# Output blocks inside key blocks, layer norm work in odd steps, and another order at the end of the attention part

## The reference

```
x = L0_attn_x
x = x + _L0_attn_ref(_layernorm(x, axis=-1), L0_attn_gamma, L0_attn_w_qkv, L0_attn_w_out)
x = x + _L0_ffn_ref(_layernorm(x, axis=-1), L0_ffn_router_w, L0_ffn_w1, L0_ffn_b1, L0_ffn_w2, L0_ffn_b2)
...
# _L0_attn_ref
xn = rms_norm(x, gamma)
qkv = xn @ w_qkv
...
sim = jnp.einsum('bhid,bhjd->bhij', q * scale, k)
attn = jax.nn.softmax(sim, axis=-1)
out = jnp.einsum('bhij,bhjd->bhid', attn, v)
...
# _L0_ffn_ref
expert_out = jnp.matmul(jax.nn.gelu(jnp.matmul(xt, w1) + b1), w2) + b2
out = expert_out * jnp.sum(combine, axis=-1, keepdims=True)
```

## Time and profile before

| | before |
|---|---|
| time, median of 3 runs (lowest to highest) | 1206.61 us (1205.59 to 1207.03) |
| the profiled execution: its own time, its span | 1207.99 us, 1206.2 us |
| busy in the span: TensorE, its weight loads | 1166.3 us (97%), 990.5 us (82%) |
| VectorE, ScalarE, GpSimd | 1008.0 us (84%), 872.4 us (72%), 660.9 us (55%) |
| mean granted TensorE clock | 0.997 |
| chain that ended last, share of TensorE | 83% |

### The profile page before, as it was taken

One profiled execution on the slowest core, in us unless ns is written; L12 is line 12 of the kernel. 1 busy time (PEld: TensorE's weight loads), 2 busy tenths in 40 slices (PEclk: granted clock), 3 DMA queues, 4 the chain that ended last, 5 costly groups with the idle time before them and its releaser, 6 DMA issues.

```text
span 1206.2 us, 26861 instructions
## 1 busy us (share of the span) xinstructions
PE 1166.3 (97%) x10171; PEld 990.5 (82%) x10171; DVE 1008.0 (84%) x1738; ACT 872.4 (72%) x1897; POOL 660.9 (55%) x826
## 2 busy tenths in 40 slices
PE   9999999999999999999999999999999988999999
PEld 6778888888788888887888788878887876898898
DVE  7888888888988888888888988898889877777764
ACT  6888877888788778877888788878887866334432
POOL 5776565655565555655565556565655576222321
PEclk9999999999999999999999999999999989999999
DMA  4232112311231123112311222121212234424421
GB/s 133 78 90 74 36 36 71 86 30 36 62 88 36 37 71 89 36 37 71 89 37 36 71 70 56 36 65 51 71 35 63 54 88 139 131 90 135 129 73 36
DMA packets 58271, 82.95 MB, mean 69 GB/s; under 512 B 12576, under 2 KB 34592, under 8 KB 58144
## 3 DMA queue, kind: packets, MB, share of 16 engines
q1 hardware_dynamic: 58144, 81.24, 24.5%
HBM read 31.14 MB, written 16.25 MB: 39 GB/s over the span
## 4 chain that ended last, share of the span: by engine, by line
PE 83%; DVE 7%; issue 2%; POOL 1%; ACT 1%; DMA 1%; SPq 0%; ACTq 0%; POOLq 0%
PE ps L609 43%; PE ps L688 18%; PE ps L636 9%; PE ps L673 8%; PE ps L642 4%; DVE xres L1179 3%; DVE xn L1158 1%; DVE nat L1162 1%; PE ps L800 1%; ACT prob L941 0%; POOL prob L1036 0%; DMA xn<-blocks_scratch 0%; DVE ln_var L1145 0%; DVE ln_stats L1138 0%; POOL attT_lo L1073 0%
## 5 line engine op out<-in xcount | busy, mean ns | idle before, releaser
L1036 POOL TENSOR_SCALAR prob<-prob,rowinv 128x512 f32<-128x512 f32 x512 | 352.5, 701 | 382.8 <-DVE rowinv L1255 382.7
L941 ACT ACTIVATE prob<-ps,negmax 128x512 f32<-128x512 f32 x512 | 347.5, 686 | 51.1 <-DVE negmax L1250 40.1
L1162 DVE TENSOR_TENSOR pT_lo<-ps,pT_hi 128x512 fp32r<-128x512 f32 (+1 forms) x384 | 320.7, 863 | 65.6 <-ACT pT_hi L934 60.0
L1250 DVE TENSOR_REDUCE negmax<-ps 128x2 f32<-128x1024 f32 x256 | 310.8, 1214 | 1.3 <-PE ps L642 1.2
L931 ACT ACTIVATE pT_hi<-ps 128x1024 fp32r<-128x1024 f32 x128 | 131.7, 1029 | 129.1 <-issue 127.8
L673 PEld LDWEIGHTS ps<-identity,prob 64*128 64x128 f32 x4096 | 159.7, 139 | 64.1 <-issue 25.0
L636 PE MATMUL ps<-nat 64*128 64x512 f32 x1024 | 175.0, 413 | 16.8 <-DVE xres L1179 13.9
L673 PE MATMUL ps<-identity,prob 64*128 64x64 f32 x4096 | 178.4, 226 | 12.1 <-DVE nat L1162 9.6
L934 ACT ACTIVATE pT_hi<-ps 128x512 fp32r<-128x512 f32 x256 | 139.6, 605 | 5.5 <-PE ps L673 1.7
L688 PE MATMUL ps<-pT_hi,vbuf 128*128 128x512 f32 x512 | 138.5, 392 | 0.5 <-DVE pT_lo L1162 0.5
L688 PE MATMUL ps<-pT_lo,vbuf 128*128 128x512 f32 x512 | 137.0, 389 | 0.0
(11 more groups left out here) (115 smaller groups left out, 2286.9 us busy)
## 6 DMA issues: line engine op xcount, KB each, us to landing
att_hi_v<-halves_out SPq DMA_DIRECT2D x128, 128.0 KB, 2.3
att_lo_v<-halves_out SPq DMA_DIRECT2D x128, 128.0 KB, 2.3
blocks_scratch<-xblocks SPq DMA_DIRECT2D x15, 512.0 KB, 3.0
xn<-blocks_scratch SPq DMA_DIRECT2D x60, 128.0 KB, 2.8
xin<-in_x SPq DMA_DIRECT2D x32, 128.0 KB, 3.0
xres<-in_x SPq DMA_DIRECT2D x8, 512.0 KB, 3.5
x_scratch<-xres SPq DMA_DIRECT2D x8, 512.0 KB, 4.4
xin<-x_scratch SPq DMA_DIRECT2D x32, 128.0 KB, 3.1
```

The costliest lines, as they stand in the source:

```text
L941: act.activation(prob[:, n % NPROB, j * SEQ:(j + 1) * SEQ], ps[:, PS_SCORE[n % 2] + j, :], ACT.Exp, bias=negmax[:, n % 4, j:j + 1], accum_ ...
L1036: return pool.tensor_scalar(dst, src, scalar, 1.0, ALU.mult, ALU.mult)
L1162: return dve.tensor_tensor(dst, full, hi, ALU.subtract)
L1250: dve.tensor_reduce(negmax[:, n % 4, :], ps[:, PS_SCORE[n % 2]:PS_SCORE[n % 2] + 2, :], AX.X, ALU.max, negate=True).then_inc(s_max, 1)
```

## The change

- **Output blocks inside key blocks.** In an even step the order is now: query block, the key block's three matmuls of the first feature half (`begin_keys`), the output block, the key block's last three matmuls. The output block has place 2 (still bank 0), the key block place 3. VectorE adds the output block before it makes the query block's low part. In step 126 the output block takes place 1, which is another bank.
- **Row maxima.** In even steps VectorE takes the maximum of tile 2s+1 right after that of tile 2s, ahead of the low part of tile 2s-2.
- **Layer norm work in odd steps.** The tasks of a batch stand in slots 6, 7, 10, 11, 14, 15, 18, 22 and 23 (`LN_SLOTS`), all of them in odd steps. Statistics are in steps 3 and 5, the normalisation in 7 and 9, both turns in 11. GpSimd's power is in step 6.
- **End splits in other steps.** GpSimd splits weight chunk 8 in step 124 ahead of tile 248, ScalarE makes the high part of chunk 9 in step 126, between the exponentials of tiles 252 and 253, and the last input's split moves from step 125 to step 126, behind tile 252 on GpSimd and to the end of the step on VectorE. The first up product of step 128 stands ahead of that step's output blocks.
- **Last output blocks** stand between the down products of tiles 1 and 2 of batch 0, in other banks. The router of batch 1 follows the up products at once. GpSimd combines the last pair after the last hidden tile, VectorE adds the blocks after it has finished the first half of batch 0, and SyncE stores that residual later in its queue.

```
-NEXT_LN_SLOT = 5
+LN_SLOTS = {6: 0, 7: 1, 10: 2, 11: 3, 14: 6, 15: 10, 18: 8, 22: 9, 23: 13}
-PS_LAST_OUT = (7, 6, 5, 4)
+PS_LAST_OUT = (7, 4, 3, 1)
...
-            blocks += [(1, "q", step // 2 + 1), (2 if step else 4, "k", step // 2 + 1)]
+            blocks += [(1, "q", step // 2 + 1), (3 if step else 4, "k", step // 2 + 1)]
...
-                blocks += [(1, "out", quarter, 0), (2, "out", quarter, 1)]
+                blocks += [(1, "out", quarter, 0), (3, "out", quarter, 1)]
             elif quarter < NPAIR // 2 - 2 and since in (0, 2):
-                blocks.append((3, "out", quarter, since // 2))
+                blocks.append((2 if step < STEPS - 2 else 1, "out", quarter, since // 2))
-            by_place = {1: odd_banks(step), 2: odd_banks(step) + 1, 3: PS_SCORE[0]}
+            by_place = {1: odd_banks(step), 2: PS_SCORE[0], 3: odd_banks(step) + 1}
...
-            return b + 1 if rel == SPLIT_STEP and 0 <= b < B else None
+            return b + 1 if rel == SPLIT_STEP + (b == B - 1) and 0 <= b < B else None
...
+            def begin_keys(step, block_no, place, kind, pair):
+                pe.wait_ge(s_ptlo, 2 * (2 * step - 3) + 2)
...
+                products(ps[:, aux_bank(block_no), :], [w[:, 0, base:base + P] for w in wqkv],
+                         [v[:, 0, :] for v in xT], True, False)
...
-                if place == 3:
+                if begun:
+                    pass
+                elif place == 2:
                     pe.wait_ge(s_exp, 2 * (2 * step) + 1)
...
-                        for k in range(KT):
+                        for k in range(1 if begun else 0, KT):
...
             def last_outs():
-                pe.wait_ge(s_halves, STEPS)
-                pe.wait_ge(s_added, added_no(NPAIR // 2 - 2, 1))
+                pe.wait_ge(s_gelu, FT)
...
-                for block_of_aux in first:
-                    aux(step, *block_of_aux)
                 if 0 <= tail < TAIL_UPS:
                     up(0, tail)
+                for block_of_aux in first:
+                    if block_of_aux[1:3] == (2, "out") and first[-1][2] == "k":
+                        begin_keys(step, *first[-1])
+                    aux(step, *block_of_aux)
...
-                if c == 0:
-                    last_outs()
                 if c + 1 < B:
                     route(c + 1)
...
                 down(c, 0)
                 down(c, 1)
+                if c == 0:
+                    last_outs()
                 down(c, 2)
...
# ScalarE
+                if step == STEPS - 2:
+                    split_weight(9)
...
# GpSimd
-                elif task and task[1] == 4:
+                elif task and task[0] and task[1] == 3:
                     powers(task[0] + 1)
...
+                if step == STEPS - 4:
+                    split_weight(8)
...
                 if 0 <= 2 * step < NUNIT:
                     normalise_prob(2 * step)
+                if split_step(step) == B:
+                    input_hi(B)
...
# VectorE
+                    if step % 2 == 0 and 0 <= 2 * step + 1 < NUNIT:
+                        row_max(2 * step + 1)
                     if 0 <= 2 * step - 2 < NUNIT:
                         transposed_lo(2 * step - 2)
-                    if 0 <= 2 * step + 1 < NUNIT:
+                    if step % 2 and 0 <= 2 * step + 1 < NUNIT:
                         row_max(2 * step + 1)
...
-                for block_of_aux in early_blocks(step):
+                for block_of_aux in sorted(early_blocks(step), key=lambda block: block[1:3] != (2, "out")):
                     aux_done(*block_of_aux)
```

54 lines of the change are left out of this document (33 added, 21 removed).

## The result

The changed kernel takes 1174.03 us (median of 4 runs, 1170.96 to 1175.16) against 1206.24 us beside it: ratio 0.9729, 95% interval 0.9709 to 0.9748. The forecast was 1171, its range 1163 to 1184. So the range held, and the forecast was 3.0 us too low.

What follows compares the result with a forecast made beforehand. TensorE, busy 1166.3 of 1206.2 us, was taken as the bound, so only shorter distances between matmul starts help. 21.2 + 11.6 + 1.5 + 1.2 = 35.5 us off 1207.99, then 1.38 lower for the median: 1171 us, range 1163 to 1184.

Steps and rivals of the forecast that it cites:

- term 1: Even steps, output block inside the key block: 0.36 us saved per pair of steps, 59 pairs, 21.2 us.
- term 4: The end, steps 126 to 129 and the hand-over to batch 1's router: 1.2 us saved, between -3 and 8.
- The stall: Scores waiting on the output block's addition in 59 even steps: 0.42 us each, expected to go.
- The gate: Even steps: output block waits for the exponential's first half on ScalarE; priced 0.06 us, between 0 and 1.86.
- all hidden: Rival: the gate opens in time and the end gives 5 us; 43 us saved, 1163 us; chance 0.12.
- The second bullet: VectorE's addition of the output block releases the scores 0.15 us before they are due, so the stall goes.
- the third: Key block's end: VectorE's key low part is released at 510.2, leaving 0.2 us before the next transposes.
- The wait changes its name: Rival: the gate costs as much as the old stall, 0.42 us; 14.3 us saved, 1192 us; chance 0.14.
- The slower rival: The exponential reaches the gate late in most steps, 1.44 us lost per pair, 1277 us; decides from 0.66; chance 0.03.
- Term 2: Layer norm work moved to odd steps: waits of 0.41 and 1.24 us go in batches 1 to 7, 11.6 us.
- Term 3: Steps 3, 5 and 7, without output block before them: earlier second maximum saves 0.5 us each, 1.5 us.
- The two waits it foresaw: Steps 126 to 129: tile 251's transposes wait about 2.2 us, values of pair 62 about 2.6, for VectorE's low parts.

Runs made afterwards that it cites:

- the run that misses the gate: Changed kernel with the output block ahead of the whole key block, three matmuls of 512 columns earlier: 1213.23 us.
- the kernel with all moves: Changed kernel with store behind regrouping, last input's high part and weight chunk 9 in GpSimd's step 126, and batch 0 down products before batch 1's router: 1167.76 us.
- the last kernel: The kernel with all moves, with the exponential of batch 1's router put behind that batch's GELUs: 1169.77 us.

## Why the prediction was right, and where it was off

| term | forecast | measured in the traces |
|---|---|---|
| 1, output inside the key block | 21.2 | 59 x 0.385 = 22.7 (a pair 15.27, now 14.885) |
| 2, layer norm in odd steps | 11.6 | 11.6, with 0.3 lost in steps 14 and 15 taken off the sum |
| 3, steps 3, 5, 7 | 1.5 | 1.3 up to step 8 |
| 4, the end | +1.2 | 0.8 - 2.1 = -1.3 |
| sum | 35.5 | 34.1 |

The sum comes nearer than its terms: term 1 gave 1.5 us more than forecast and term 4 2.5 less, and that these cancel in part is luck.

*Term 1.* The stall went, 0.42 of 0.42. The gate was priced at 0.06 us and took about 0.05, though by another way than the prediction had it. It put 0.15 us of release behind ScalarE's half; the run that misses the gate shows 0.06 (ScalarE ends at 524.01, the block starts at 524.07). So the gate opens at about 504.26, and the block's first matmul starts on time at 504.31 (in 58 of the 59 pairs). Its second starts 0.17 behind it (504.48), where it was 0.11 to 0.12 before and is 0.12 in step 126, where ScalarE is done 3.5 us earlier. In all 59 pairs that second matmul comes 0.27 to 0.28 us behind ScalarE's end, whatever the first had to spare, and so it does in the run that misses the gate. So "all hidden" did not happen. Two things were left out, both priced at nothing. The 9 + 12 + 3 matmuls in three pieces take 2.17 + 1.49 + 0.79 = 4.45 us where two pieces took 4.37: 0.07 before rounding, of which 0.05 are the gate's. And the transposes ahead of the value block take 0.58 in place of 0.62 (+0.04, which the run with the old order of maxima gives back). The second bullet (the addition) and the third (0.2 us to spare for the key part; measured 0.4 with 0.15 for the release) held. "The wait changes its name" is refuted: a missed gate costs its lateness (0.62 us, and 0.06 in the seams), and here it is all but met. The slower rival's point of 0.66 us a pair was set too high: the change gains 32.2 us with the gate as it is, so 32.2 / 59 = 0.55 more a pair would take it all back, and with 0.68 the time was 1213 against 1206.

*Term 2.* By itself it gave 11.2 us in the body, 12.0 without what steps 14 and 15 lost, and the odd steps hold all of the work. With the rule of the Trainium skill (SBUF — State Buffer, Who interferes with whom) the prediction had 3 us to be lost. The trace has the mechanism and not that price. The moved normalisation and GpSimd's work beside it:

```profile
439.04 1.11 DVE L1185 TENSOR_SCALAR xn<-xin,ln_mv,ln_scale 128x256 f32<-128x256 f32 x2
```

```profile
438.57 1.44 POOL L1059 TENSOR_SCALAR prob<-prob,rowinv 128x512 f32<-128x512 f32 x2 [1.14 <-DVE rowinv L1282]
```

Two tiles take 1.11 us as the first two did: instruction by instruction, the first takes 0.41, as it does with GpSimd at rest, and the second 0.79. It begins 0.12 us behind GpSimd's second instruction of 0.77 and ends 0.15 behind that one's end. In the earlier trace rows the same holds for the one instruction of 1.29 us, and the two took 2.22. So the neighbour's length sets the price, and in the odd steps the neighbours are short. The step that failed is a smaller one: "GpSimd reads it only some 8 us into step 12. Nothing waits." In batch 1 it does wait, 1.3 us here, where store, a weight chunk and the regrouping leave one right behind another (97.66 to 101.3).

*Term 3* was right, 1.5 us by the run without it. TensorE's waits in these steps changed their name on the way (0.97, 0.55 and 0.55 us for a low part of a transposed tile).

*Term 4* had the wrong sign, and is where the sum was lost: two steps of its working failed. "I carry this on to 30.8 us for the stretch" gave 2.3 us, 1.5 with half clock taken off; measured 0.8. The two waits it foresaw came (1.88 and 2.08 us of idle), and they nearly fill the place of those that went: 4.6 us of idle time before, 4.0 after. The 0.8 us for half clock was the term that was too small. Behind the two waits the scores take 2.71 us in place of 1.48 and the values of pair 62 5.43 in place of 3.63, 3.0 us in all, where the same reckoning gives 2.5 before (output block, transposes and scores from 988.06 to 994.11). How the 30.8 was added up is not written down, so what else is in it stays open. VectorE's low part also took 2.77 us for its two pieces beside GpSimd:

```profile
954.52 2.77 DVE L1189 TENSOR_TENSOR xT_lo<-xn,xT_hi 128x512 fp32r<-128x512 f32 x2 [1.49 <-POOL xT_hi L1059]
```

"It waits 3.2 us or a little more: -0.3 by the difference" became 4.48 and -2.1:

```profile
989.54 1.89 PE L814 MATMUL ps<-nat,rw_parts 128*16 128x512 f32 x4 [4.48 <-DVE nat L1189]
```

The low part was to be ready 9.56 us behind the router of batch 0, as before (1014.74 to 1024.3). It was ready 10.95 behind it (978.54 to 989.49). TensorE's steps had become shorter, but the chain that makes this input (normalisation, turning, two transfers, ScalarE, VectorE) had not: its turned blocks leave 0.05 us behind the router in place of 0.88 ahead. That chain is 1.4 of what TensorE lost, but not the whole account. By the distances between starts, TensorE loses 1.6 us more by waiting at this place than before, and 1.9 by the clock (below), and it gets 1.5 back that the prediction had not seen: the up products of batch 1 no longer wait. They took 12.36 us before, with these two waits, and take 10.91 now:

```profile
1042.57 0.50 PE L609 MATMUL ps<-nat,wbig_hi 128*128 128x512 f32 x1 [0.23 <-ACT prob L956]
1048.94 0.50 PE L609 MATMUL ps<-nat,wbig_hi 128*128 128x512 f32 x1 [0.63 <-ACT prob L956]
```

1.6 + 1.9 - 1.5 is the 2.1 but for rounding. No run puts the last output blocks back alone, so this account rests on the rows.

*The medians.* The profiled run of before lies 1.75 us above its median, that of after 0.16 below. The forecast took 1.38 off, so 1.5 of its 3.0 us are no mechanism at all, and the rest is the sum's (1.4).

## What to carry to other kernels

A wait that a producer misses by little is worth an interleaving: some matmuls of a block that is ready go in front of the gated one, and the price of missing the gate is close to the lateness (0.68 us for 0.62 here), so count how many matmuls cover it. Where two waits follow each other, their prices don't add: each hides part of the other, and the second grows when the first goes. Before a wait is worked on, check its releaser: it must end ahead of the start that it released, and the kernel must wait for it there. At the hand-over between two stages an order that shortens TensorE's part must also shorten the chain of transfers behind it; otherwise the gain comes back as a wait, and here at half clock as well.

## What the runs showed of the hardware

**The clock behind a wait.** From 986 to 988 TensorE does nothing in the changed kernel, and the granted clock falls:

```profile
986.00:988.00 2.00, 0.00 (x0) 0.00 (x0) 0.11 (x1) 1.19 (x2) 1.91 (x3) 0.75 0.26 39
988.00:990.00 2.00, 0.46 (x2) 0.18 (x3) 2.00 (x2) 1.15 (x1) 1.92 (x2) 0.50 0.53 145
990.00:992.00 2.00, 2.00 (x8) 1.34 (x7) 1.97 (x4) 0.00 (x0) 0.62 (x1) 0.50 0.48 133
992.00:994.00 2.00, 2.00 (x12) 2.00 (x11) 1.50 (x11) 0.23 (x1) 0.00 (x0) 0.54 0.00 0
994.00:996.00 2.00, 2.00 (x19) 2.00 (x19) 1.90 (x7) 0.00 (x0) 0.00 (x0) 1.00 0.00 0
```

It stays at 0.50, the lower level of 1.2 GHz, while TensorE works fully from 990 on, and is 1.00 again from 994; 12 matmuls run in 2 us there, 19 at full clock. The router takes 1.68 us (989.54 to 991.22) in place of 0.94, and the 48 matmuls behind it 6.90 (to 998.12), where they take 5.76 at 0.12 each: the wait of 4.48 us cost **1.9 us more** in this way. The wait of 2.79 us at this place before left the clock at 1.00.

The length of a wait alone does not tell. In step 126 of the changed kernel the clock falls behind one of 1.88 us (ahead of 952.43), and again behind one of 2.08 (ahead of 958.70):

```profile
952.00:954.00 2.00, 1.57 (x20) 1.39 (x22) 1.03 (x3) 2.00 (x6) 1.46 (x3) 0.72 0.00 0
954.00:956.00 2.00, 2.00 (x16) 1.51 (x14) 1.48 (x2) 0.85 (x2) 2.00 (x3) 0.50 0.00 0
960.00:962.00 2.00, 2.00 (x6) 1.51 (x6) 2.00 (x3) 1.53 (x5) 2.00 (x2) 0.50 0.00 0
```

And the same wait of 2.84 us left the clock at 1.00 in the kernel with all moves (1002 to 1004), but was followed by 0.50 in the last kernel. So a planned wait of 2 us or more should be priced both ways.

**GpSimd and VectorE.** The last hidden low part of batch 0 in the kernel with all moves takes 1.78 us where its like takes 0.69, beside an addition of GpSimd that had begun 0.06 us ahead of it:

```profile
983.62 1.78 DVE L1190 TENSOR_TENSOR pT_lo<-prob,pT_hi 128x512 fp32r<-128x512 f32 x1 [0.51 <-POOL pT_hi L1071]
```

```profile
983.56 1.30 POOL L1093 TENSOR_TENSOR att_hi_v<-att_hi_v,att_lo_v 128x512 f32<-128x512 f32 x1
```

0.06 + 1.78 is the 1.30 of the one and 0.54 for the other. The low parts of this form that begin while GpSimd works bear it out in the same trace: with 0.55, 0.34 and 0.25 us of GpSimd's instruction left they take 1.09, 0.88 and 0.79. Each ends 0.54 behind the end of GpSimd's. So what counts is what is left of GpSimd's instruction, not a factor: whoever schedules beside GpSimd should look at the length of its instructions.
